# Transformer layers on one core: the first layer norm in two halves of x, the weights in two lots, the filter product and a memset at other places

## The reference, cut to what matters

```python
x = x + linear_attention(layernorm(x))   # 16 heads of 8: exp(k) cumulated, softmax(q), y @ w_out
x = x + experts(layernorm(x))            # 8 experts, each takes its top 129 tokens of a sequence, gelu
x = x + attention(layernorm(x))          # 16 query heads, one key/value head, causal softmax
x = x + filter(layernorm(x))             # fft along the columns, @ w, real part of ifft, + bias
```

## Time and profile before

| | us |
|---|---|
| runs | 750.51, 752.53, 751.91 |
| median | 751.91 |
| the profiled execution | 752.71 |
| its span | 751.0 |

### The profile page before, as it was taken

The page is one execution under the profiler, slowest core; times in us unless marked ns, Lnnn a source line. Parts: engine busy times, 40 slices in busy tenths (PEclk is TensorE's granted clock), DMA queues, the critical chain, the costliest instruction groups (busy, mean ns, idle before and its releaser), DMA issues.

```text
span 751.0 us, 14209 instructions
## 1 busy us (share of the span) xinstructions
PE 618.1 (82%) x4111; PEld 369.9 (49%) x4111; DVE 521.4 (69%) x1779; ACT 374.9 (50%) x800; POOL 391.2 (52%) x529
## 2 busy tenths in 40 slices
PE   2478888888405999999799778999999999999894
PEld 1235555554302688776566533545454545444453
DVE  8458888887794112225478859898989898987554
ACT  0322333331450423326622357777777777767873
POOL 0077777776004777776887554343434343433341
PEclk9989999999855999999999989999999999999997
DMA  9400000000040122244663244040304030200011
GB/s 297 133 0 1 1 0 0 0 1 0 16 140 28 49 43 39 39 93 84 110 98 35 26 82 53 10 59 10 59 10 60 9 60 9 60 5 2 24 52 42
DMA packets 45145, 34.55 MB, mean 46 GB/s; under 512 B 4304, under 2 KB 41728, under 8 KB 45072
## 3 DMA queue, kind: packets, MB, share of 16 engines
q1 hardware_dynamic: 33584, 25.15, 14.5%
q0 software_dynamic: 10144, 7.90, 7.5%
q10 hardware_dynamic: 1344, 0.62, 0.3%
HBM read 14.13 MB, written 9.70 MB: 32 GB/s over the span
## 4 chain that ended last, share of the span: by engine, by line
PE 46%; DVE 16%; issue 8%; ACT 4%; POOL 1%; DMA 1%; DVEq 0%; ACTq 0%; POOLq 0%
PE bank L2146 8%; PE wide L1275 6%; DVE masked L1744 6%; PE wide L2133 5%; PE wide L2082 5%; PE wide L1283 4%; PE bank L1283 4%; PE bank L2082 2%; PE wide L2158 2%; ACT L282 1%; DVE mx L1744 1%; DVE slot_t L886 1%; POOL x_row L1045 1%; PE bank L2057 1%; PE bank L1300 1%
## 5 line engine op out<-in xcount | busy, mean ns | idle before, releaser
L1941 ACT ACTIVATE pexp<-wide 128x512 f32<-128x512 f32 (+2 forms) x384 | 180.9, 536 | 77.9 <-PE wide L2133 75.9
L1744 DVE CUSTOM_DVE_ANT_0 masked<-wide,mask_qk 128x128 f32<-128x128 f32 (+3 forms) x423 | 182.8, 477 | 46.9 <-PE wide L2082 46.1
L1872 POOL TENSOR_SCALAR_AFFINE_SELECT pexp<-pexp 128x256 f32<-128x256 f32 x256 | 106.4, 429 | 166.7 <-ACT pexp L1941 165.2
L2133 PE MATMUL wide<-qT,kTe 128*128 128x256 bf16 (+3 forms) x512 | 121.8, 301 | 6.1 <-ACT pexp L1941 3.7
L2082 PE MATMUL wide<-kTm,qT 128*128 128x128 bf16 (+3 forms) x423 | 102.6, 300 | 13.2 <-DVE mx L1744 10.8
L1036 POOL DMA_INDIRECT x_dram<-yg,row_u x56 | 89.4, 1597 | 30.6 <-DVE yg L1088 15.7
L1225 ACT ACTIVATE hT<-wide,b1T 128x512 f32<-128x512 f32 x64 | 43.9, 686 | 100.7 <-PE wide L1275 100.7
L1045 POOL DMA_INDIRECT x_row<-xln_dram,row_u x64 | 62.6, 978 | 52.5 <-DVE slot_tok L915 33.6
L2146 PE MATMUL bank<-pexp,vx 128*32 128x512 f32 (+3 forms) x1024 | 85.4, 446 | 4.9 <-POOL pexp L1872 4.9
L2133 PEld LDWEIGHTS wide<-qT,kTe 128*128 128x128 bf16 x512 | 48.6, 99 | 42.5 <-ACT pexp L1941 23.1
L1275 PE MATMUL wide<-xgT,w_sb 128*128 128x512 f32 x128 | 67.4, 612 | 1.5 <-ACT xgT L1218 1.5
(11 more groups left out here) (282 smaller groups left out, 1046.6 us busy)
## 6 DMA issues: line engine op xcount, KB each, us to landing
qT<-qp SPq DMA_DIRECT2D x126, 64.0 KB
x_sb<-in_L_attn_x SPq DMA_DIRECT2D x8, 256.0 KB, 6.7
w_sb<-in_L_ffn_w SPq DMA_DIRECT2D x1, 2048.0 KB, 13.1
xln_dram<-hT SPq DMA_DIRECT2D x8, 256.0 KB, 2.3
x_dram<-x_sb SPq DMA_DIRECT2D x7, 256.0 KB, 2.7
x_sb<-x_dram SPq DMA_DIRECT2D x7, 256.0 KB, 3.1
out_x<-x_sb SPq DMA_DIRECT2D x7, 256.0 KB, 2.3
qT<-qp_first SPq DMA_DIRECT2D x18, 64.0 KB
```

Of the source, the lines that this page charges most:

```text
L1744: ins = nc.vector.tensor_tensor_reduce(out=masked[:, n % 4, at], in0=bank_of(n)[:, at], in1=mask_qk[:, T - w:T], scale=1.0, scalar=LEAST, ...
L1872: nc.gpsimd.affine_select(out=pexp[:, at, :, 0:P], in_=pexp[:, at, :, 0:P], pattern=[[0, 2], [1, P]], compare_op=ALU.is_ge, fill=0.0, base ...
L1941: nc.scalar.activation(pexp[:, exp_slot(b, 2 * step + h // 2), h % 2:h % 2 + nh, 0:w], scores_bank(b, m)[:, 0:nh * w].rearrange("p (h t) - ...
L2133: ins = nc.tensor.matmul(scores_bank(b, m)[:, hh * w:(hh + 1) * w], kTe[:, par, j * P:(j + 1) * P], qT[:, b % QB, 4 * qd + h + hh, j * P:T ...
```

## The change

DVE's memset of `qT` at the start is taken out; its three parts (one for each of the three q buffers) stand behind `yg` of phases 1, 2 and 4. The first norm is done in two parts: statistics, root, reciprocal and shift for sequences 0 to 3, and the same for sequences 4 to 7 later. DVE's order becomes: half the statistics, copies of `wqT` and `rT`, the shift of the first half, the other copies, the other half of the statistics, and in turn 0 the filter's evacuations behind qmax and the second shift behind `den`. ACT takes the second root, with two more presets, behind `qe` of turn 0. ACT's first three weights (`w_qkv`, router, `w_out`) get a signal of their own, `s_wq`, for which PE's first four transposes wait; the other seven stay on `s_w`. The filter product goes to `bank[6]` and to PE's place behind the first projection.

```diff
@@ prep_act
                 (wq_raw[:, :, :], w_qkv.rearrange("(g p) d -> p g d", p=P)),
+                (r_raw[:, :], router_w),
                 (wo_sb[:, 0:D], w_out),
-                (r_raw[:, :], router_w),
+            ):
+                q.dma_start(dst, src).then_inc(s_wq.sem, 16)
+            for dst, src in (
                 (b2_raw[:, :], b2),
...
@@ prep_pe
-            pe.wait_ge(s_w.sem, s_w.total(16 * NW))
+            pe.wait_ge(s_wq.sem, s_wq.total(16 * NWQ))
             for g, place in ((1, 0), (0, 1), (2, 2)):
                 nc.tensor.transpose(bank[0][:, place * D:(place + 1) * D], wq_raw[:, g, :], ident)
-            nc.tensor.transpose(bank[1][:, 0:E], r_raw[:, :], ident[0:E, 0:E])
+            nc.tensor.transpose(bank[5][:, 0:E], r_raw[:, :], ident[0:E, 0:E]).then_inc(s_prep_t.sem, 1)
+            pe.wait_ge(s_w.sem, s_w.total(16 * (NW - NWQ)))
...
-            pe.wait_ge(s_prep_v.sem, s_prep_v.total(4))
-            nc.tensor.matmul(bank[5][:, 0:D], a12[:, 0, :], dft_c, start=True, stop=False)
-            nc.tensor.matmul(bank[5][:, 0:D], a12[:, 1, :], dft_ns, start=False, stop=True).then_inc(s_prep_t.sem, 1)
-            pe.wait_ge(s_prep_v.sem, s_prep_v.total(6))
+        def prep_pe_filter(pe):
+            nc.tensor.matmul(bank[6][:, 0:D], a12[:, 0, :], dft_c, start=True, stop=False)
+            nc.tensor.matmul(bank[6][:, 0:D], a12[:, 1, :], dft_ns, start=False, stop=True).then_inc(s_prep_t.sem, 1)
             nc.tensor.matmul(bank[7][:, 0:E], center, rT, start=True, stop=True).then_inc(s_prep_t.sem, 1)
...
+        def prep_dve_first(dve):
+            dve.wait_ge(s_prep_t.sem, s_prep_t.total(1))
+            nc.vector.tensor_copy(wqT[:, 0:3 * D], bank[0][:, 0:3 * D]).then_inc(s_prep_v.sem, 1)
+            nc.vector.tensor_copy(rT, bank[5][:, 0:E]).then_inc(s_prep_v.sem, 1)
...
+        half_x = lambda half: slice(half * B // 2, (half + 1) * B // 2)
+        def ln1_dve_stats(dve, half):
+            dve.wait_ge(s_x[half].sem, s_x[half].total(16 * B // 2))
+            for i in range(2 * half, 2 * half + 2):
+                ln1.dve_sequences(dve, i, 2)
+            dve.wait_ge(ln1.mv.sem, ln1.mv.total(2 * half + 2))
+            nc.vector.tensor_scalar(sd[:, half_x(half), :], mv[:, half_x(half), :, 1], EPS, None,
+                                    ALU.add).then_inc(ln_ve.sem, 1)
+        def ln1_act_std(act, half):
+            act_preset(act, ACT.Sqrt)
+            act.wait_ge(ln_ve.sem, ln_ve.total(1 + half))
+            nc.scalar.activation(sd[:, half_x(half), :], sd[:, half_x(half), :], ACT.Sqrt).then_inc(ln_sd.sem, 1)
+            act_preset(act, ACT.Exp)
+        def ln1_dve_shift(dve, half):
+            at = half_x(half)
+            dve.wait_ge(ln_sd.sem, ln_sd.total(1 + half))
+            nc.vector.reciprocal(rstd[:, at, :], sd[:, at, :]).then_inc(ln_rstd.sem, 1)
+            dve.wait_ge(ln_rstd.sem, ln_rstd.total(1 + half))
+            nc.vector.scalar_tensor_tensor(out=shift1[:, at, :], in0=mv[:, at, :, 0], scalar=-1.0, in1=rstd[:, at, :],
+                                           op0=ALU.mult, op1=ALU.mult).then_inc(s_shift.sem, 1)
...
@@ lin_dve
             dve_lin_qmax(dve, 0, 0)
+            prep_dve_filter(dve)
             dve_lin_qsum(dve, 0)
             dve_lin_den(dve, 0)
+            ln1_dve_shift(dve, 1)
             prep_dve_logits(dve)
@@ lin_act
             act_lin_qe(act, 0)
+            ln1_act_std(act, 1)
             act_lin_turn(act, 0, 0, tail=False)
             act_lin_turn(act, 1, 1)
+            act.wait_ge(s_shift.sem, s_shift.total(2))
@@ lin_pe
+            pe.wait_ge(s_prep_v.sem, s_prep_v.total(1))
             pe_lin_xT(pe, 0, first=True)
+            pe.wait_ge(s_prep_v.sem, s_prep_v.total(6))
             for k in range(NT):
                 pe_lin_qkv(pe, 0, k)
+            prep_pe_filter(pe)
             pe_lin_key_sums(pe, 0, 0, first=True)
@@ moe_dve, ZERO_AT = (1, 2, 4)
                 dve_moe_gated(dve, p)
+                if p in ZERO_AT:
+                    nc.vector.memset(qT[64:P, ZERO_AT.index(p)], 0.0).then_inc(s_zero.sem, 1)
@@ mqa_sync
-            sp.wait_ge(s_zero.sem, s_zero.total(2))
+            sp.wait_ge(s_zero.sem, s_zero.total(1 + QB))
@@ vector program
             nc.vector.memset(kTm[64:P, :, :], 0.0).then_inc(s_zero.sem, 1)
-            nc.vector.memset(qT[64:P, :, :, :], 0.0).then_inc(s_zero.sem, 1)
             dve.wait_ge(s_started, LIN)
-            for i in range(B // 2):
-                if i % 2 == 0:
-                    dve.wait_ge(s_x[i // 2].sem, s_x[i // 2].total(16 * B // 2))
-                ln1.dve_sequences(dve, i, 2)
-            ln1.dve_var_eps(dve, B // 2)
-            prep_dve(dve)
-            ln1.dve_inverse(dve)
-            nc.vector.scalar_tensor_tensor(out=shift1[:, :, :], in0=mv[:, :, :, 0], scalar=-1.0, in1=rstd[:, :, :],
-                                           op0=ALU.mult, op1=ALU.mult).then_inc(s_shift.sem, 1)
+            ln1_dve_stats(dve, 0)
+            prep_dve_first(dve)
+            ln1_dve_shift(dve, 0)
+            prep_dve(dve)
+            ln1_dve_stats(dve, 1)
             lin_dve(dve)
```

More of the change, by code:

```diff
@@ L105, in build @@
         lg = sb("lg", [P, B, NT, E])
-        preset = sb("preset", [P, 16])
+        preset = sb("preset", [P, 20])
         wo_sb = sb("wo_sb", [P, D + E])
@@ L172, in build @@
         s_w = signal("weights_loaded", 1, 16)
+        s_wq = signal("first_weights_loaded", 1, 16)
         s_we = signal("expert_weights_loaded", 1, 16)
         s_c = signal("consts_loaded", 1, 16)
-        NW = 10
+        NW, NWQ = 10, 3
         NWE = 3
@@ L180, in build @@
         s_prep_v = signal("prep_evacuated")
-        s_idb = signal("ident_bf_ready")
         s_zero = signal("unused_rows_zeroed")
@@ L266, in prep_dve, with prep_dve_filter @@
             nc.vector.tensor_copy(b2T[:, :], bank[1][:, E:2 * E]).then_inc(s_prep_v.sem, 1)
-            dve.wait_ge(s_prep_t.sem, s_prep_t.total(2))
-            nc.vector.tensor_scalar(m_sb[:, :], bank[5][:, 0:D], 1.0 / D, None, ALU.mult).then_inc(s_prep_v.sem, 1)
+        def prep_dve_filter(dve):
             dve.wait_ge(s_prep_t.sem, s_prep_t.total(3))
+            nc.vector.tensor_scalar(m_sb[:, :], bank[6][:, 0:D], 1.0 / D, None, ALU.mult).then_inc(s_prep_v.sem, 1)
+            dve.wait_ge(s_prep_t.sem, s_prep_t.total(4))
             nc.vector.tensor_copy(rTc[:, :], bank[7][:, 0:E]).then_inc(s_prep_v.sem, 1)
         def prep_dve_logits(dve):
-            dve.wait_ge(s_prep_t.sem, s_prep_t.total(4))
+            dve.wait_ge(s_prep_t.sem, s_prep_t.total(5))
             nc.vector.tensor_copy(wo_sb[:, D:D + E], bank[7][:, E:2 * E]).then_inc(s_prep_v.sem, 1)
-        preset_column = iter(range(16))
+        preset_column = iter(range(20))
         def act_preset(act, func):
@@ L329, in act_std @@
                 nc.scalar.activation(sd[:, :, :], sd[:, :, :], ACT.Sqrt).then_inc(self.sd.sem, 1)
-        ln1, ln2, ln3, ln4 = (LayerNorm(f"ln{n}", n) for n in range(1, 5))
+        ln1, ln2, ln3, ln4 = (LayerNorm(f"ln{n}", n if n == 1 else n + 1) for n in range(1, 5))
+        half_x = lambda half: slice(half * B // 2, (half + 1) * B // 2)
[18 more added lines that the diff above has]
+                                           op0=ALU.mult, op1=ALU.mult).then_inc(s_shift.sem, 1)
         A = lambda name, per=1: signal("lin_" + name, per)
@@ L1189, in moe_dve @@
             dve_moe_gated(dve, E)
-            dve_inverse(dve, 0, 1, 3)
+            dve_inverse(dve, 0, 1, 4)
             dve_ln3_shift(dve, 0, 1)
@@ L1197, in moe_dve @@
             dve_moe_gated(dve, E + 1)
-            dve_inverse(dve, 1, G, 4)
+            dve_inverse(dve, 1, G, 5)
             dve_ln3_shift(dve, 1, G)
@@ L1583, in dve_end_xln @@
             token = lambda a: a.unsqueeze(2).broadcast_to([P, END_TILES, D])
-            dve.wait_ge(ln_sd.sem, ln_sd.total(8 + half))
+            dve.wait_ge(ln_sd.sem, ln_sd.total(9 + half))
             nc.vector.reciprocal(rstd[:, B - 1, end_tiles(half)], sd[:, B - 1, end_tiles(half)]).then_inc(ln_rstd.sem, 1)
             nc.vector.tensor_tensor(to, part, token(mv[:, B - 1, end_tiles(half), 0]), ALU.subtract).then_inc(f_c.sem, 1)
-            dve.wait_ge(ln_rstd.sem, ln_rstd.total(8 + half))
+            dve.wait_ge(ln_rstd.sem, ln_rstd.total(9 + half))
             dve.wait_ge(f_c.sem, f_c.at(B - 2, half + 1))
@@ L1602, in act_end_std @@
         def act_end_std(act, half):
-            act.wait_ge(ln_ve.sem, ln_ve.total(8 + half))
+            act.wait_ge(ln_ve.sem, ln_ve.total(9 + half))
             nc.scalar.activation(sd[:, B - 1, end_tiles(half)], sd[:, B - 1, end_tiles(half)], ACT.Sqrt).then_inc(ln_sd.sem, 1)
@@ L1852, in mqa_dve @@
             dve_var_eps(dve, ln4, B - 2, B - 1)
-            dve_inverse(dve, B - 2, B - 1, 7)
+            dve_inverse(dve, B - 2, B - 1, 8)
             dve_end_shift(dve)
@@ L1967, in act_turn @@
                 if (b, s) == (0, SECOND_STD_STEP):
```

(7 more changed lines are left out.)

22 lines of the change are left out of this document (10 added, 12 removed).

## The result

The changed kernel takes **739.27 us** (median of 4 runs, 739.08 to 741.22) against 752.22 for the kernel before in the same session: ratio 0.9838, 95% interval 0.982 to 0.9856. Its profiled execution took 739.08 with a span of 737.3. Forecast were 738.3 for the median and 737.4 for the span.

The account below looks back on a forecast made before the run. VectorE's early work that the first linear-attention turn doesn't need (qT clearing, half the statistics, filter) was taken to delay it. 12.95 (start) + 0.62 (clock) = 13.57 us, from median 751.91 to 738.3 us; range 735.0 to 743.9.

Parts of the forecast that it names:

- The start of the first turn: First normalized tile starts at 14.58 instead of 27.53 us, without the qT memset and half the statistics ahead: 12.95 us.
- the late start: Rival, chance 0.10: the start signal or x reaches VectorE only with the constants; gain 11.39 + 0.62, 739.9 us.
- Hidden as forecast: Second half of the statistics, other weight copies, filter products and second root fit into waits up to the first product: zero cost.
- GpSimd's signals: Rival, chance 0.03: GpSimd needs 36.7 us for 115 signals before its first work, so keys start as late; some 751.4 us.
- The clock: Turn 0: the filter fills TensorE's idle, so the last key sums (L688) run at 2.4 GHz: 0.62 us less.
- Passed down: Later turns wait only for the turn before, so the 12.95 us pass unchanged to the routing and the experts.
- The memsets: Three pieces behind phases 1, 2 and 4 of the experts, 4.27 us each: zero; without cover 12.8 us.
- The 0.36 us: Second memset moves phase 3's buffers and `place` into 3.91 us idle before L1085, which it may delay by 0.36 us.
- The held-scatters rival: Rival, chance 0.12: memsets hold GpSimd, its scatters start late, the last by 5.6 us: 743.9 us.
- its doubled form: Rival, chance 0.02: the same hold with nothing absorbed, each piece costing 5.88 us, 17.6 in all: 755.9 us.
- pricing lost cover: If VectorE's idle among the experts did not cover the three memsets, they would cost 3 x 4.27 = 12.8 us.

Follow-up runs that it names:

- two sequences first: Changed kernel with the norm's first part two sequences instead of four, x in three lots, constants issued behind the second: 736.03 us, ratio 0.9801.
- the run with one lot: Changed kernel with TensorE's first transposes waiting for all ten weight loads, as before the change: 739.45 us.
- filter early: Changed kernel with the filter product and VectorE's copies of it back ahead of the first projection: 739.99 us.
- the repeated run: Changed kernel run again with only a comment line added: 739.65 us, ratio 0.9846.
- the run with the memsets alone: Kernel before with only the qT memset moved, as three memsets among the experts: 747.52 us, ratio 0.9943.
- two memsets: Changed kernel with each of the three qT memsets among the experts doubled: 744.86 us, ratio 0.989.
- the run with three: Changed kernel with two more memsets of the same size ahead of each of the three among the experts: 762.25 us, ratio 1.0124.
- two sequences first and the fourteen products: Changed kernel with a first norm part of two sequences, x in three lots, and fourteen unread TensorE products in gaps of turn 0: 736.07 us.

## Why the prediction was right, point by point

**The start of the first turn** was forecast as 12.95 us and measured 12.80. x released VectorE at 8.06 instead of 7.8; half the statistics took 4.83 to L346 (forecast 4.79 and 0.03); from there to the end of the preset it was 1.93 (1.96), and `xln` starts 0.09 before that end. The rival of the late start is out: VectorE was released by x, not by the start signal, and with two sequences first it began at 5.51, so the signal is there by then. The table switch cost what its row says, with the next ACTIVATE right behind; no trace here has the drain of the Trainium skill (ScalarE: Activation LUTs, section What ACT_TABLE_LOAD costs).

**Hidden as forecast:** the second half of the statistics, done at 19.86 (21.3 forecast) for a qmax at 24.02 (24.3); the copies of the second lot, 15.16 (16.5 at the latest); ScalarE's second root, with 3.36 us left; GpSimd's signals, since its keys came 13.23 us earlier. That the first transposes start at the constants' landing is true and, as the run with one lot shows, worth nothing.

**The clock** was forecast as 0.62 us in L688's successor; that row gave 0.52. Another 0.53 came from the projection (5.06 for 5.59), of which 0.43 reached `den` (28.38 for 42.13: 13.75, less the 12.80 of the start and the 0.52). So 0.95, with the outer sums still slow, as the forecast had it. For the key sums the mechanism is borne out by most traces, not by all (filter early, above). The projection's share is luck: the forecast has no term for it, the same program took 5.31 to 5.57 us there in the repeated run and in those with more memsets, and the old order took 4.97 in the run with the memsets alone. A premise was off: the filter took 0.74 us at the new place, not 1.45, and left 1.59 us of the wait rather than 0.7.

**Passed down.** The distance is 13.75 us at `prod` 0, 13.65 at `prod` 1, 13.66 at the first MAX8, 13.60 at the first `yg` and 13.7 at the end, of 13.57 forecast. So no more than 0.15 was given back on the way.

**The memsets** cost nothing. Each took 4.38 us by row and idle (4.27 forecast; the row shows 3.47). The `yg` of phase 3 came at 275.45; its row of before, less the 13.60, is 275.44; the `rest_r` of phase 5 came at 298.49, its row of before less the 13.60 is 298.48. TensorE was busy without a gap from 243 to 330. The 0.36 us by which the second might have been late left out the idle ahead of `place` in the kernel before:

```profile
284.64 0.49 DVE L1097 TENSOR_SCALAR place<-tokens_f,slot_tok 128x512 f32<-128x512 f32 x1 [0.74 <-PE wide L1293]
```

So the cover was 4.65 us, not 3.91. POOL's scatters kept their 1.6 us. The held-scatters rival and its doubled form are out, as the Trainium skill (SBUF — State Buffer, section Who interferes with whom) has it for a VectorE instruction with at most one SBUF input. The forecast named `place` as the first thing an overrun would delay; with two memsets it was `yg` and the 129th token's item. And pricing lost cover by the memsets' own time was too cheap: in the run with three, 9.5 us of waits cost 23.0 us (762.25 less 739.27), since TensorE's clock fell with them.

**The median** came 1.0 us above the forecast while the span fitted to 0.1: the profiled execution of before lay above its median, that of after 0.2 below its own. That the span fitted so well is in part chance: the start gave 0.15 less than forecast and the clock 0.33 more, mostly by the projection's pace, and the repeated run's span is 0.6 longer (737.9).

## What to carry to other kernels

Find what the first link waits for and count only the work that it needs: here half of a norm was enough, a quarter was better, and the loads' order then set the bound. A filler goes where its engine waits for a busy one, and its size is that wait: one piece cost nothing, two already overran. If the busy engine is TensorE, price an overrun at more than the wait, because the clock may fall with it and stay down behind it. Differences of one or two us can't be read from one profiled run when the clock's falls, 1.6 us each, move between runs.

## What was not expected

**A small VectorE operation can be held by GpSimd.** The second shift took 1.23 us where the first, of the same shape, took 0.17; the first stands alone, the second began 0.07 us behind GpSimd's `qs` (32.54, 1.27 us) and ended with it. All the profiled runs with the split norm have 1.2 us there. It cost nothing, since `prod` needs `qs` anyway. The Trainium skill (SBUF — State Buffer, section Who interferes with whom) says that a VectorE instruction with two SBUF inputs contends with a GpSimd instruction that reads SBUF; the two rows agree.

**The first projection's pace varies from run to run:** 5.06, 5.31, 5.55 and 5.57 us, but 3.19 with two sequences first and the fourteen products, while the granted clock reads 1.00 in these windows in all of them:

```profile
17.02 3.19 PE L720 MATMUL wide<-wqT,xT 128*128 128x392 f32 x8 [0.73 <-issue]
```

A turn later it takes 3.22. So the column doesn't show the slow pace at the beginning, and the rows have to be read instead. The Trainium skill (TensorE: Matmul & The Clock Gate, Part 1) says that the same kernel changes its level at another matmul from run to run; these rows agree.
